# Attention: ten unread products before the first scores of each unit, and row transfers issued in slots 6 and 4

## The reference, cut to what matters

```python
h = tok(x)                                  # 64 images x 196 tokens x 192
h = h + attn(_layernorm(h))                 # layer 0: 12 heads of 16
h = h + ffn(_layernorm(h))                  # ffn begins with layer 1:
    # h = _ln(x, ln1_g, ln1_b); q, k, v = split(h @ in_w.T + in_b)
    scores = einsum('bqhd,bkhd->bhqk', q, k) / sqrt(D)
    attn = softmax(scores); ctx = einsum('bhqk,bkhd->bqhd', attn, v)
    x = x + ctx @ out_w.T + out_b           # then an MLP and four experts
```

## Time and profile before

| | |
|---|---|
| median of 3 runs | 3173.27 us (3169.94 to 3174.86) |
| profiled execution | 3171.36 us, span 3169.6 us |
| granted TensorE clock, mean | 0.947 |
| attention phase, both layers | from about 400 to about 1850 us of the span |
| half-clock stretches between 450 and 1820 us | ten, 61.2 us |
| PE busy | 2756.1 us (87% of the span) |

### The profile page before, as it was taken

One profiled execution on the slowest core, in us unless ns is written; L12 is line 12 of the kernel. 1 busy time (PEld: TensorE's weight loads), 2 busy tenths in 40 slices (PEclk: granted clock), 3 DMA queues, 4 the chain that ended last, 5 costly groups with the idle time before them and its releaser, 6 DMA issues. The chain is left out here.

```text
span 3169.6 us, 95506 instructions
## 1 busy us (share of the span) xinstructions
PE 2756.1 (87%) x31491; PEld 2128.4 (67%) x31491; DVE 2320.9 (73%) x5326; ACT 1878.0 (59%) x3798; POOL 1671.7 (53%) x1957
## 2 busy tenths in 40 slices
PE   4999379998999988989998858988984999999998
PEld 3888345555555555555555538888874888888887
DVE  4888477887878787878787726766655777777776
ACT  3888256676666666666666637666642444444443
POOL 2777325455554666666666441556554444444444
PEclk8999688999999999999999969999986999999999
DMA  5564245667666666677767635444433444444443
GB/s 140 162 188 125 58 111 136 157 151 161 147 153 151 157 165 160 159 170 163 162 162 164 152 81 139 135 128 132 129 107 95 67 67 67 68 67 67 67 67 50
DMA packets 515433, 395.07 MB, mean 125 GB/s; under 512 B 223136, under 2 KB 488386, under 8 KB 515138
## 3 DMA queue, kind: packets, MB, share of 16 engines
q1 hardware_dynamic: 431426, 310.47, 40.2%
q0 software_dynamic: 38496, 46.38, 8.3%
q10 hardware_dynamic: 45216, 34.34, 4.6%
HBM read 232.59 MB, written 155.42 MB: 122 GB/s over the span
## 5 line engine op out<-in xcount | busy, mean ns | idle before, releaser
L701 DVE TENSOR_REDUCE a_mx<-a_mxp 98x4 f32<-98x784 f32 x768 | 747.5, 973 | 278.5 <-PE a_mxp L850 275.3
L540 ACT ACTIVATE a_pt<-a_st 98x784 f32<-98x784 f32 x768 | 633.9, 825 | 364.9 <-PE a_st L836 363.8
L1609 POOL DMA_INDIRECT out_dram<-f_yo,f_idg x202 | 329.8, 1633 | 417.2 <-DVE f_yo L1950 380.7
L481 POOL TENSOR_TENSOR a_cf<-a_ctxs,a_rec 128x1176 f32<-128x1176 f32 x64 | 171.5, 2680 | 456.1 <-DMA a_rec<-a_recip 456.1
L1687 ACT ACTIVATE f_hf<-f_bank,f_b1c 128x256 f32<-128x256 f32 x606 | 253.9, 472 | 236.5 <-PE f_bank L924 236.3
L865 PE MATMUL a_pv<-a_pt,a_vp 98*32 98x196 f32 x6144 | 359.6, 353 | 5.4 <-issue 4.4
L836 PE MATMUL a_st<-a_qst,a_kst 49*128 49x196 f16 x3072 | 268.1, 254 | 78.8 <-DMA a_qst<-a_mrow 54.2
L2112 PE MATMUL f_bank<-f_w2h,f_hh 128*128 x1212 | 298.9, 247 | 14.4 <-DVE f_hl L1934 13.0
L2113 PE MATMUL f_bank<-f_w2h,f_hl 128*128 x1212 | 298.2, 246 | 0.0
L2114 PE MATMUL f_bank<-f_w2l,f_hh 128*128 x1212 | 298.2, 246 | 0.0
L850 PE MATMUL a_mxp<-a_kst,a_qst 48*128 48x196 f16 x3072 | 264.9, 251 | 27.5 <-DVE a_mx L701 22.7
(11 more groups left out here) (324 smaller groups left out, 8367.6 us busy)
## 6 DMA issues: line engine op xcount, KB each, us to landing
a_rec<-a_recip SPq DMA_DIRECT2D x256, 147.0 KB, 4.9
t_rows<-in_x_dram SPq DMA_DIRECT2D x84, 392.0 KB, 5.9
a_qst<-a_qk SPq DMA_DIRECT2D x256, 110.2 KB, 3.1
a_kst<-a_qk SPq DMA_DIRECT2D x256, 110.2 KB, 3.8
f_xg<-f_listed SPq DMA_DIRECT2D x101, 264.0 KB
a_qk<-a_qkh SPq DMA_DIRECT2D x128, 196.0 KB, 3.1
a_qk<-a_qkl SPq DMA_DIRECT2D x128, 98.0 KB, 3.4
a_qk<-a_qkh SPq DMA_DIRECT2D x128, 98.0 KB, 2.5
```

What stands on the lines that cost most here:

```text
L540: act.activation(pt[k % PT][:].rearrange("p j a t -> p j (a t)"), st_ps[0:half_t, :, 0:unit_t], ACT.Exp, scale=sm_scale).then_inc(exp_s, 1)
L701: dve.tensor_reduce(mx[:, a, :, 2 * p:2 * p + 2].rearrange("p q j -> p j q"), mx_ps[0:half_t, :, 0:unit_t].rearrange("p j (q t) -> p j q t ...
L1609: pool.indirect_dma_start(out, bass.IndirectOffsetOnAxis(ap=idg[i % 3][:, t:t + 1], axis=0), yo[i % 3][:, t, :], None, compute_op=ALU.add) ...
```

## The change

ScalarE issues the store of a_xx behind slot 4 in place of slot 0 (so behind the transfers of maxima of slot 3), and the load of a_xres behind slot 6 in place of slot 8. PE computes ten products of 256 columns ahead of the scores of slot 0; they write columns 256 to 511 of the bank of a_pv, which nobody reads, from weights that are always there, and wait for nothing.

```diff
@@ ScalarE, step
                     empty(k, 0)
-                    if k == 0 and kinds.get("L") == 1:
+                    if k == 3 and "C" in kinds:
+                        place_maxima(s, par, 1)
+                    if k == 4 and kinds.get("L") == 1:
                         u = s + 3
                         wait(act, xx_s, 4 * (u - UL + 1))
                         act.dma_start(of_units(r_rows, u, 1), xx[:]).then_inc(res_s, 16)
-                    if k == 3 and "C" in kinds:
-                        place_maxima(s, par, 1)
-                    if k == 8 and "O" in kinds:
+                    if k == 6 and "O" in kinds:
                         u, b = s - 1, (par + 1) % 2
                         waits(act,
                               (xo_s, OUTS * (u - 1) + 1),
@@ TensorE, step
+                    if k == 0 and "C" in kinds:
+                        keep_busy(10)
                     if "C" in kinds:
                         scores(s, par, k)
...
+            def keep_busy(n):
+
+                for _ in range(n):
+                    pe.matmul(pv_ps[:, 256:512], wh[0][:, 0, 0:128], wh[0][:, 0, 0:256], start=True, stop=True)
```

## The result

The changed kernel is slower: 3189.60 us (median of 20 runs, 3167.40 to 3221.43) against 3174.11 us (20 runs, 3164.59 to 3193.34) for the kernel before, a ratio of 1.0052 with a 95% interval of 1.0032 to 1.0072. I had forecast 3141 and faster. Its profiled execution took 3190.95 us, span 3189.1.

What follows compares the result with a forecast made beforehand. The attention was taken as bound by TensorE, with its waits and half clock. Terms +16 -10 -7 +5 -9 -23 gave -28 us, so 3145, put at 3141 as the shorter unit avoids some half-clock stretches; range 3115 to 3205.

Steps and rivals of the forecast that it cites:

- How much earlier does a_cf start? ... I take 2.3: Residual load in slot 6: POOL's a_cf starts 2.3 us earlier, bounds 0 and 3.0.
- the second quiet place: a_cf starting 2.4 to 3.3 us before the border, where VectorE's a_negm leaves PE little or no gap; 2.8 forecast.
- Products* +16: Border: ten products before each of 64 units cost 77 us and hide 61 us of waiting for the maxima; net +16.
- a_cn* -10: PE's projection no longer waits for POOL's a_cn: 8 us, and -10 taken with the weight loads that stand too.
- a_mx* -7 and +5: Turned scores waiting for VectorE's maxima: -7 us from gaps gone, +5 from new gaps where a_cf's lead falls to 2.2.
- a_xo and a_sums* -9: Store in slot 4, second layer: a_sums earlier, so the slot 6 projection waits less for a_xo; -9 us, bounds -13 and +10.
- I cost that at nothing: Residual load in slot 6 meeting SP's a_qst loads and a_qk stores (slots 6 to 8): no cost taken.
- Clock* -23: PE's 61.2 us at half clock: 12 us back after long border waits, 11 from the others; -23, bounds 0 and -31.
- Rival 1: a_cf starts where a_ch or a_cn blocks a_negm in most units: 3243 us, or 3200 for a quarter; chance 0.2.
- Rival 2: Transfers move nothing, as the maxima may queue behind SP's loads of the next unit: 3190 us; chance 0.09.
- Rival 3: Products do nothing for the clock, 12 us less gained: 3155 us; chance 0.18 together with Rival 4.
- Rival 4: Store in slot 4 meets a_xin and a_sums, +10 in place of -9: 3160 us; chance 0.18 together with Rival 3.

## Why the prediction was wrong

**The step that failed** is "How much earlier does a_cf start? ... I take 2.3" and the place that it gave, "it becomes 2.8, the second quiet place". From the first a_rec issue to a_cf it was 7.44 us in the mean of 58 units and is 5.59: 1.85 us, well within the bounds of 0 and 3.0, but nearly half a microsecond short of what I took. The 3.0 came from the unit of the earlier trace rows, where the loads of the next unit are missing too; I knew that and still went three quarters of the way. With the border 0.2 us later for the products the lead is 2.38 in place of 2.8, where my own rule (gap = 4.9 less lead less 2.1) gives 0.4 us in the middle unit and over 0.7 from a lead of 2.1 down. "A quarter of 60 units at 0.3: +5" became 48 waits of 0.59 us. The run with 14 products bears the rule out: at the forecast's lead the waits for a_mx (7.6 us) and the half clock (13.6 us) are no more than forecast. It does not bear out the sum: four more products cost 28 us, which the forecast of -28 would just have covered, and the median is 13 us above the kernel before.

**The terms.** *Products* +16: 61 units at 1.19 less the 60 us that they cover, +13. Right in size; but the two transfers alone remove the wait too, so the products covered one that would have been gone. *a_cn* -10: PE's row is gone, 5.9 us. *a_mx* -7 and +5: +12.5 us of waits, some 6 after what is made up (0.3 in each of 20 more). *a_xo and a_sums* -9: -1. The store alone does bring it (0.3%), but "I cost that at nothing", of the residual load beside SP's a_qk transfers, was the second wrong step: I looked for its readers on PE, and the one that waited was SP itself, with a_sums behind it. *Clock* -23: 68.2 for 61.2 us at half clock, +3.5; the falls behind border waits are gone, and as many more came behind the a_mx gaps. 13 - 6 + 6 - 1 + 3.5 is +15.5. That the medians differ by 15.5 too is luck: the terms are read from two profiles, whose attention differs by 12.0, and in the second profile of the changed kernel half clock is 57.9 us, which turns the last term's sign. What is safe is that of the 23 us at most 2 came. This is the largest gap between the sum and the measurement, some 25 of 43 us, and it hangs on the step above, as eleven of the twelve falls came behind a_mx gaps.

The runs with a_negm on ScalarE show what the change is worth where no a_mx gap can arise: 0.9954 with it and 0.9946 without, each to 0.0025, so no gain. By their profiles the products are +13, a_cn -8 (8.8 to 0.6 us), a_xo +2, and half clock falls by 7 us only. So even with the lead made harmless nothing like -28 was to be had: the gaps and most of the half clock go by moving a_negm alone, and the wait for the maxima is paid back in products.

**The rivals.** Rival 1 is what happened, in a milder form than priced: three quarters of the units blocked, not by 0.9 us but by 0.6, because the lead (2.38) lay just past the far edge of its stretch. Without the products it is that rival in full. Its point of decision, about ten units, can't be tested: 48 units stood, and twelve stretches followed, where the kernel before had ten. Rival 2 is wrong, the residual load moves the maxima and a_rec. Rival 3, that products do nothing for the clock, stays open: half clock is least where few waits of 0.7 us or more are left, with products (13.6 and 17.0 us) and without (23.8), and nothing here separates the products' own part. Rival 4 (the store makes a_sums late) is out, as the store alone shows; a_sums does come late, but with the residual load moved. My range held the time; the chance of 0.2 for rival 1 was too low, as the bounds on a_cf's start, 0 to 3.0, put a third of their width into its stretch.

## What to carry to other kernels

When a transfer is moved so that an engine starts earlier, ask what that engine's instructions will then meet, and treat a shift of known sign but uncertain size as a draw between good and bad places: here 0.4 us made the difference between 28 us of waits and 8, and taking a_negm off VectorE removed the draw. A wait that goes away on one path shows up on the next longest one; look for it on the in-order queues of the issuing engines too, where a wait for a landing holds up issues that don't depend on it, and fill it by reordering. When a gain is forecast at one wait, ask what the change is worth with the rival's cause taken away: here, with a_negm on ScalarE, it was worth nothing. Extra work can act as a delay (the two transfers cost 1.4% without the products and 0.5% with them): change its amount before believing in another reason.

## What the runs showed of the hardware

VectorE's small a_negm (98x24, 0.17 us alone) took up to 2.33 us in the changed kernel, where a GpSimd instruction had started 0.13 us before it, and 0.18 us where it started 0.05 us ahead of one; on ScalarE it took 0.21 to 0.25 us throughout. In the changed kernel TensorE's granted clock fell to 0.50 for 3.4 or 6.8 us behind single idle times of 0.67 to 1.79 us, in stretches where PE was otherwise busy; idle times of 0.95 us there, and of 1.20 us with 14 products (unit at 571.92), passed without a fall. The Trainium skill ("TensorE: Matmul & The Clock Gate", HAM oscillation — how this bites in real kernels) ties such falls to longer idle times; no run here shows why ones as short as these are enough. With a 294 KB load issued on ScalarE's queue ahead of them, the a_qk stores on SP's queue (196 and 98 KB) took 4.0 and 4.2 us to land, where they took 3.1 and 3.6 (means of 58 units, residual load alone against the kernel before).
